# Moving the sixth x tile and the second x2 tile forward in the opening of an attention and FFN kernel

## What is computed

```
x  = x + xattn(layernorm(x), ctx)          # 4096 rows of 512, 8 heads of 128
x  = x + ffn(layernorm(x))

xattn: q = xn Wq, k = ctx Wk, v = ctx Wv   # 154 context rows, seen by all rows
       sim = (q k') * scale, stretched around its mean by 1.5
       out = softmax(sim) v Wout + bout
ffn:   xr = mu_r x + (1 - mu_r) x_prev     # x_prev is the row before
       xk = mu_k x + (1 - mu_k) x_prev
       out = sigmoid(xr W_r') * (relu(xk W_k')^2 W_v')
```

## Time and profile before

| | |
|---|---|
| median of 3 runs | 759.24 us (758.82 to 760.24) |
| profiled execution, its own time | 759.64 us |
| profiled execution, span from first to last instruction | 757.9 us |
| TensorE busy | 745.9 us, 98% of the span |
| VectorE, ScalarE, GpSimd busy | 510.4, 425.7, 121.4 us |
| mean granted clock of TensorE, share of full speed | 0.995 |

### The profile page before, as it was taken

The page is one execution under the profiler, slowest core; times in us unless marked ns, Lnnn a source line. Parts: engine busy times, 40 slices in busy tenths (PEclk is TensorE's granted clock), DMA queues, the critical chain, the costliest instruction groups (busy, mean ns, idle before and its releaser), DMA issues.

```text
span 757.9 us, 13608 instructions
## 1 busy us (share of the span) xinstructions
PE 745.9 (98%) x3996; PEld 651.9 (86%) x3996; DVE 510.4 (67%) x1071; ACT 425.7 (56%) x1199; POOL 121.4 (16%) x279
## 2 busy tenths in 40 slices
PE   8999979999999999999999999999999999999998
PEld 8976869888888989898888988888898989888887
DVE  2658677677776666777666667776766677766762
ACT  3667556464665755465565646466475646555332
POOL 1110011211112121210202121111212121020211
PEclk9999998999999999999999999999999999999999
DMA  9933444543544454444535454344445444443301
GB/s 313 339 105 113 142 128 136 167 129 111 164 120 134 145 167 138 129 138 131 159 93 173 139 166 133 108 158 131 131 136 167 137 127 142 128 147 105 107 30 42
DMA packets 84072, 106.28 MB, mean 140 GB/s; under 512 B 9775, under 2 KB 61001, under 8 KB 84043
## 3 DMA queue, kind: packets, MB, share of 16 engines
q1 hardware_dynamic: 84043, 105.92, 44.4%
HBM read 58.44 MB, written 47.45 MB: 140 GB/s over the span
## 4 chain that ended last, share of the span: by engine, by line
PE 90%; DVE 4%; ACT 3%; issue 1%; POOL 1%; DMA 0%; POOLq 0%; DVEq 0%; ACTq 0%; SPq 0%
PE ffn L470 11%; PE ffn L472 11%; PE ffn L471 11%; PE scores L471 9%; PE scores L472 9%; PE scores L470 9%; PE attended L472 8%; PE attended L471 8%; PE attended L470 8%; ACT probs L756 1%; PE scores L650 1%; PE attended L508 1%; PE attended L507 1%; ACT probs L765 1%; PE scores L681 1%
## 5 line engine op out<-in xcount | busy, mean ns | idle before, releaser
L471 PE MATMUL scores<-A_lo,xT_hi 128*128 128x462 f32 (+1 forms) x384 | 134.5, 350 | 0.0
L470 PE MATMUL scores<-A_hi,xT_hi 128*128 128x462 f32 (+1 forms) x384 | 134.2, 349 | 0.0
L472 PE MATMUL scores<-A_hi,xT_lo 128*128 128x462 f32 (+1 forms) x384 | 134.1, 349 | 0.0
L756 ACT ACTIVATE probs<-scores,neg_max 128x154 f32<-128x154 f32 x256 | 96.2, 386 | 42.8 <-DVE neg_max L1005 39.4
L1005 DVE TENSOR_REDUCE neg_max<-scores 128x3 f32<-128x462 f32 (+1 forms) x96 | 55.5, 583 | 87.0 <-PE scores L472 87.0
L472 PE MATMUL attended<-B_hi,pT_lo 128*128 128x512 f32 x288 | 112.4, 390 | 0.0
L471 PE MATMUL attended<-B_lo,pT_hi 128*128 128x512 f32 x288 | 112.3, 390 | 0.0
L470 PE MATMUL attended<-B_hi,pT_hi 128*128 128x512 f32 x288 | 112.0, 389 | 0.0
L1264 POOL TENSOR_SCALAR var<-stats 128x1 f32<-128x1 f32 x64 | 12.2, 191 | 465.6 <-DVE stats L952 464.5
L470 PE MATMUL ffn<-xk_hi,WkT_hi 128*128 128x256 f32 x256 | 73.7, 288 | 5.3 <-DVE xk_lo L946 5.3
L470 PEld LDWEIGHTS scores<-A_hi,xT_hi 128*128 128x128 f32 x384 | 72.4, 189 | 7.3 <-issue 0.8
(11 more groups left out here) (177 smaller groups left out, 1567.7 us busy)
## 6 DMA issues: line engine op xcount, KB each, us to landing
prob_rows<-probs SPq DMA_DIRECT2D x32, 704.0 KB, 3.4
probs_handed<-prob_rows SPq DMA_DIRECT2D x128, 176.0 KB, 3.3
x_rows<-normed SPq DMA_DIRECT2D x61, 256.0 KB, 2.0
handed<-x_rows SPq DMA_DIRECT2D x244, 64.0 KB, 1.9
x_in<-in_x SPq DMA_DIRECT2D x32, 256.0 KB, 3.5
out<-x SPq DMA_DIRECT2D x31, 256.0 KB, 2.4
wq<-in_L_xattn_Wq SPq DMA_DIRECT2D x4, 512.0 KB, 8.6
wout<-in_L_xattn_Wout SPq DMA_DIRECT2D x1, 2048.0 KB, 16.1
```

The lines of the kernel that those rows point to most:

```text
L470: te.matmul(psum, left[0], right[0], start=first, stop=False)
L471: te.matmul(psum, left[0], right[1], start=False, stop=False)
L472: return te.matmul(psum, left[1], right[0], start=False, stop=last)
L756: last = nc.scalar.activation(probs[:, q, cols], S[b][:, (h - h0) * J:(h - h0 + 1) * J], ACT.Exp, bias=neg_max[:, h:h + 1], accum_out=row_ ...
```

## The change

Nothing is computed differently; the order is. TensorE's own stream has the same instructions in the same order. Three things move:

- Tile 5 of x gets a second early buffer (where x2 of slot 2 will be), is loaded by one more DMA in the opening, and is normalised, stored, handed and transposed in the opening too. Its residual rows are still loaded into `x_in` as before, so the kernel reads 256 KB more.
- `step(0, 2)` of ScalarE and VectorE is written out (`from_second=True` skips it in `turns`): the mixture of tile 1 comes first, and `maxima(4)` and all of P(4) behind it. `hand_x2(1)` is issued ahead of `hand_probs(3)`.
- The scaling and packing of P(0) stand ahead of the rounding of W_r.

The steps' own calls for x of tile t+3 now ask `comes_in_steps(t + 3)`, which leaves tiles below 6 out.

```diff
-        x_early = sb("x_early", [P, D], at=at_x2 + 3 * size_of([P, D]))
+        x_early = [sb(f"x_early{i}", [P, D], at=at_x2 + (3 - i) * size_of([P, D])) for i in range(2)]
@@ SyncE
+            sp.dma_start(x_early[1][:], xt[5 * P:6 * P, :]).then_inc(early_loaded[1], 16)
@@ hand_x
                 if begun(t - 5):
-                    sp.wait_ge(xn2T_ready, t - 3)
+                    sp.wait_ge(xn2T_ready, 1 if isinstance(t, int) and t == 5 else t - 3)
@@ hand_x2
-                if not begun(t - 1):
-                    sp.wait_ge(x_turned, 5)
-                elif begun(t - 2) and is_tile(t + 3):
+                if not begun(t - 2):
+                    sp.wait_ge(x_turned, t + 5)
+                elif is_tile(t + 3) and not (isinstance(t, int) and t == 2):
                     sp.wait_ge(x_turned, t + 4)
@@ SyncE, opening
             store_probs(2)
+            store_x(5)
             load_x(4, 0)
...
             load_x(5, 1)
+            hand_x(5)
             store_x2(1)
+            hand_x2(1)
             hand_probs(3)
-            hand_x2(1)
@@ ScalarE, opening
+            normalise_early(0)
+            pack_hi(0)
             for n in range(4, 8):
                 weights_hi(n)
-            normalise_early(0)
-            pack_hi(0)
...
             pack_hi(2)
+            x_norm(5, None)
             x2_norm(0, 0)
...
                 probs_hi(2, i)
+            x_hi(5)
             mixed_high("k", 0, 0)
             mixed_high("r", 0, 0)
-            turns(act_e, step)
+            mixed_high("k", 1, 1)
+            exponentials(4, 0)
+            mixed_high("r", 1, 1)
+            exponentials(4, 1)
+            exponentials(4, 2)
+            normalise_early(4)
+            pack_hi(4)
+            open_gate(0, 0, 2)
+            x2_norm(2, 2)
+            for i in range(3):
+                probs_hi(3, i)
+            squares(0, 0)
+            turns(act_e, step, from_second=True)
@@ VectorE, opening
+            normalise_late(0)
+            pack_lo(0)
             for n in range(4, 8):
                 weights_lo(n)
-            normalise_late(0)
-            pack_lo(0)
...
                 maxima(2, b)
+            x_statistics(5, None, 1)
...
+            x_turn(5)
             dve.wait_ge(mu_loaded, 32)
             mix(0, 0, 0)
             mixed_low("k", 0, 0)
             mixed_low("r", 0, 0)
-            turns(dve, step)
+            x2_turn(1, 1, 0)
+            mix(1, 1, 0)
+            mixed_low("k", 1, 1)
+            for b in range(3):
+                maxima(4, b)
+            x_lo(5)
+            mixed_low("r", 1, 1)
+            inverse_early(4)
+            normalise_late(4)
+            pack_lo(4)
+            add_x(2, 0, 2)
+            probs_turn(3)
+            for i in range(3):
+                probs_lo(3, i)
+            turns(dve, step, from_second=True)
@@ GpSimd, opening
             x_root(4)
+            x_root(5)
```

More of the change, by code:

```diff
@@ L214, in xattn_ffn @@
             sem("consts_ready"), sem("rows_zeroed"), sem("high_marked"), sem("rows_marked"))
-        early_loaded = sem("early_loaded")
+        early_loaded = [sem(f"early_loaded{i}") for i in range(2)]
         ctxT_turned, ctx_summed, ctx_shifted, ctxT_keys_ready, ctxT_ready = (
@@ L277, in place, with comes_in_steps, turns @@
             return 4 * g + s, 2 * g + s // 2 - 1, s % 2
-        def turns(eng, step):
-            step(0, 2)
+        def comes_in_steps(t):
+            return is_tile(t) and not (isinstance(t, int) and t < 6)
+        def turns(eng, step, from_second=False):
+            if not from_second:
+                step(0, 2)
             step(0, 3)
@@ L339, in _ @@
             load_rows(raw_w["r"], W_r, ffn_loaded["r"])
-            sp.dma_start(x_early[:], xt[4 * P:5 * P, :]).then_inc(early_loaded, 16)
+            sp.dma_start(x_early[0][:], xt[4 * P:5 * P, :]).then_inc(early_loaded[0], 16)
             load_rows(raw_w["v"], W_v, ffn_loaded["v"])
@@ L418, in step @@
                 t, q, half = place(g, s)
-                if is_tile(t + 3):
+                if comes_in_steps(t + 3):
                     store_x(t + 3)
@@ L727, in x_norm @@
                 to = x_view((normed, normed2)[t]) if turned_by_pe(t) else by_quarter(normed)
-                rows = x_in[slot] if slot is not None else x_early
+                rows = x_in[slot] if slot is not None else x_early[t - 4]
                 rows = x_view(rows) if turned_by_pe(t) else in_quarters(rows)
@@ L955, in x_statistics @@
                 if slot is None:
-                    dve.wait_ge(early_loaded, 16)
+                    dve.wait_ge(early_loaded[t - 4], 16)
                 else:
@@ L960, in x_statistics @@
                     dve.wait_ge(shift1_ready, t)
-                statistics(x_in[slot] if slot is not None else x_early, raw1, stats1, raw1_ready, stats1_ready, t)
+                statistics(x_in[slot] if slot is not None else x_early[t - 4], raw1, stats1, raw1_ready, stats1_ready, t)
             def turn_blocks(dst, src, width):
```

## The result

The changed kernel takes 754.57 us (median of 4 executions, 754.2 to 754.75), the kernel before 759.03 (4 executions beside it). The ratio is 0.994, with a 95% interval of 0.9927 to 0.9952. It is 4.5 us faster. The forecast was 752.2, with a range of 750.0 to 755.0. In the profiled executions the span went from 757.9 to 752.9 us.

The account below looks back on a forecast made before the run. TensorE, busy 98% of the span, was taken as the bound. Span: 757.9 - 0.8 - 8.04 + 1.8 = 750.9; from the median, 759.24 - 7.0 = 752.2 us, range 750.0 to 755.0.

Parts of the forecast that it names:

- the case that the forecast took for the likely one: One new TensorE wait of 1 to 3 us at key_columns(1), giving 751.4 to 753.4 us; chance 0.5.
- the new wait: TensorE waiting for xk_lo at key_columns(1), because VectorE and ScalarE come only 0.9 us earlier against TensorE's 8.04; +1.8 us.
- First term, P(0): In the opening, P(0) ahead of W_r brings B's casts sooner and buys nearly all of TensorE's B_lo wait; -0.8 us.
- Tile 5 at no cost: Tile 5's opening work falls into engine pauses; x_turn(5) takes 0.7 us of VectorE without delaying TensorE; costed at nothing.
- the risk that was named and left out of the sum: hand_x(5) queued behind other SyncE transfers, so tile 5's rows land late for x_turn(5); 753.9 to 755 us, chance 0.15.
- Second term: At key_columns(0), tile 1's xk is ready in time, so TensorE's 5.34 us wait and its 2.70 us half-clock cost vanish; -8.04 us.
- What is late next: The chain from step(0, 3) through x_norm(7) and x2_turn(3) to xk_lo, ready 153.7 with key_columns(1) due 151.9; +1.8 us.
- the clock falls in the new wait: Rival: TensorE's clock halves in the 1.8 us wait at key_columns(1), bringing back 2.70 us, 754.9 us; chance 0.1.
- the long wait: TensorE's 5.3 us wait for xk_lo at key_columns(0) in the kernel before, priced at 8.04 us with its half clock.

Follow-up runs that it names:

- root_first: The changed kernel with the root of tile t+3 ahead of the second add of the pair before in GpSimd's step; 752.18 us.
- exps_first: The changed kernel with the exponentials of tile t+2 ahead of x_norm(t+3) in ScalarE's steps for the first tile of a pair; 751.28 us.
- after_filled_8: The changed kernel with 8 extra identity matmuls, results unused, between gate_rows(1, 0) and key_columns(1); 752.66 us.
- p0_only: The kernel before with only P(0)'s scaling and packing moved ahead of W_r's rounding; 757.79 us.
- no_p0: The changed kernel without the move of P(0)'s scaling and packing ahead of W_r's rounding; 754.34 us.
- before_filled_24: The kernel before with 24 extra identity matmuls, results unused, between gate_rows(0, 0) and key_columns(0); 756.97 us.
- before_filled: The kernel before with 46 extra identity matmuls, results unused, between gate_rows(0, 0) and key_columns(0); 761.87 us.

## Why the prediction was right, and where it was off

The measured time lies in the range, but not in the case that the forecast took for the likely one (751.4 to 753.4): the change won 4.5 us where 7.0 were forecast. The order of the engines, the waits and where they move were forecast rightly; the clock in the new wait was not.

- **First term, P(0).** Forecast -0.8; measured -0.83 in the profile (`scores(2)` from 63.85 to 63.02). The first exponential came at 51.64, forecast 51.7. Right.
- **Tile 5 at no cost.** The statistics, the root and `x_norm(5)` fell into the pauses named. `x_turn(5)` cost its 0.7, and 0.27 more in waiting for its DMA [98.76 above], the risk that was named and left out of the sum. Its four transfers landed in 2.2 to 2.6 us, between the undisturbed 1.8 to 2.0 of x2's in the same profile and the 3.2 I had allowed.
- **Second term.** Forecast -8.04; measured -7.81. `xk_lo` was ready for 107.89; on the kernel before's own clock of events (0.83 later) that is 108.7 against the forecast 108.4. The difference is 0.3 us of waiting left over, nearly all of it the 0.27 us of the DMA ahead of `x_turn(5)`.
- **What is late next.** All links came within 0.3 us of the forecast once the 0.83 of the opening are taken off, which the chain of forecasts leaves out: `x2_turn(2)` forecast 127.8, less 0.8 is 127.0, measured 127.30; `xT_lo(6)` 133.8 and 134.1; `x_norm(7)` 144.7 and 144.92; the wait 1.8 and 1.93. root_first and exps_first show that it was this chain: shortened by one link, it cut the wait to 1.04 us, by another, to nothing. That it ends with this pair is right too: no further wait stands in the profile.
- **The clock, the step that failed.** The rival "the clock falls in the new wait" got a chance of 0.1 and nothing in the sum. It happened in all four executions (mean clock 0.997 to 0.998), and cost 1.58 us in the profile and 1.9 by after_filled_8. The argument against it was that 1.8 us is shorter than the 4.4 after which it had fallen, and that a wait of 0.83 had not lowered it. Neither bears: p0_only shows the fall 2.1 us into the same wait of 5.34; no_p0 shows a wait of 2.54 without a fall and, in two other executions without a profile, a mean clock and a time that look like one. One row of a fall tells when it happened once, not what it takes. The rows at hand left it open, so the chance belonged nearer to one half than to one in ten.
- The size of that rival was off as well: 2.70 were forecast if it came, by the long wait's example, and 1.58 came, since the stretch at half clock was 3.4 us here and 6.8 there. With -4.97 measured in the span, the forecast of -7.04 lacks 1.58 for the clock, 0.2 at `key_columns(0)` and 0.3 for the wait at `key_columns(1)`. The 0.3 us that are left to the difference of the medians come from the profiled executions, which are not the median ones.
- The time came out at the upper part of the range because this rival was in it. The range covered it; the chance of 0.1 did not see it coming. And the 754.9 of that rival is close to 754.57 by luck: its price was 1.1 us too high, and the waits, which came out longer, and the executions made up for most of that.
- One reading of the waits was incomplete: TensorE also waits 1.5 us for `identity` at the start of the span, in both kernels, and the change does not touch it. The granted clock is 1.00 in every us of the first eight of the kernel before.

The Trainium skill's page TensorE: Matmul & The Clock Gate (A second HAM failure mode) tells of another kernel, in which frequent micro-idles between groups of matmuls made the clock go up and down. It is near to this case but not the same: here a single wait of 1.93 us was followed by one fall, and the 0.83 us wait for `B_lo` by none.

## What to carry to other kernels

When TensorE is made to come earlier, compute how much earlier each of the other engines comes at the same place. The difference is a debt that the next tight chain presents: here 8.0 against 0.9 us and a wait of 1.9 us 45 us later. Look then for an instruction in that chain that does not belong to it: swapping `x_norm` of a later tile behind the exponentials was worth 3.3 us, where the whole change was worth 4.5. And price a new wait of TensorE as the wait plus a possible stretch at half clock, even where a shorter wait and a longer one in the trace seem to speak against it: 1.93 us cost another 1.58 here.

## What the runs showed of the hardware that was not expected

- Whether the clock falls in the wait at `key_columns(1)` differs from one execution to the next of the same kernel (no_p0, 2.54 us in the profile: 753.6 to 754.3 at a mean clock near 1.0, 756.4 at 0.998). The wait of 1.04 us in root_first left it at 1.00 in all four executions. In the long wait of the kernel before it fell every time, as mean clocks of 0.998 and less say, but at another moment, after 2.1 us (p0_only's profile) or after 4.4 us (the kernel before's). In p0_only the executions at 0.995 took 758.1 to 758.8 us and those at 0.998 took 757.2 to 757.5.
- Filling a wait with 1.95 us (after_filled_8) or 5.5 us (before_filled_24) of useless matmuls kept the clock at 1.00 and gained about 2 us; filled with twice as much, the gain was gone.
- A 128x128 matmul of the identity in float32 by `matmul` costs 0.22 us and shows as two records (before_filled); a transposing one of the same size steps by 0.11 us (in the kernel before, twelve for W_q take from 15.28 to 16.59).
